# Pass two's score units moved next to pass one's, one addition moved from VectorE to GpSimd, and one early wait dropped

## What is computed

```python
xn  = layernorm(x)
# 1. rotary attention, 16 heads of 8, with a decay bias
q, k, v = heads(xn @ Wqkv.T);  q, k = rotate(q), rotate(k)
s   = q @ k.T / sqrt(8) - |i - j| / xi * e_g          # causal
a1  = (softmax(s) @ v) @ Wo.T
# 2. "soft mixture" attention: 8 experts gate the projections
n1  = layernorm(xn) * ln1_w + ln1_b;  rw = gating(n1)  # (tokens, 8)
q   = sum_e (n1 * rw_e) @ q_proj[e]   # k, v alike
hs  = xn + sum_e (softmax(q @ k.T / sqrt(128)) @ v * rw_e) @ o_proj[e]
# 3. mixture of 8 experts on the result
n2  = layernorm(hs) * ln2_w + ln2_b;  rw2 = gating(n2)
out = x + a1 + hs + sum_e (gelu(n2 @ w1[e]) @ w2[e]) * rw2_e
```

## Time and profile before

| | |
|---|---|
| median of 3 runs | 1262.35 us |
| the profiled execution | 1263.52 us, its span 1261.7 us |
| granted TensorE clock, mean | 0.985 |
| PE, PE weight load, DVE, ACT, POOL busy | 93%, 71%, 82%, 56%, 18% of the span |
| first matmul of step 0 / of the expert stage | 66.64 us / 1016.84 us |
| chain that ended last, by engine | PE 45%, DVE 29%, issue 15%, ACT 7%, the rest 4% |

### The profile page before, as it was taken

How to read it: one execution, slowest core, us unless ns; L and a number is a source line. 1 busy time by engine, 2 the same in 40 slices (tenths; PEclk the granted TensorE clock), 3 DMA queues, 4 the chain that set the end, 5 groups by cost and what they waited for, 6 DMA issues and landing times.

```text
span 1261.7 us, 33146 instructions
## 1 busy us (share of the span) xinstructions
PE 1177.7 (93%) x10652; PEld 899.4 (71%) x10652; DVE 1030.4 (82%) x3704; ACT 710.2 (56%) x1286; POOL 220.9 (18%) x338
## 2 busy tenths in 40 slices
PE   2399999999999999999999999999999899999998
PEld 1167777777777777777777777777777677777776
DVE  8878888888888888888888888888876667777664
ACT  2155565665666666655666666666665744555532
POOL 4212222222222222222222222222223000000000
PEclk9789999999999999999999999999999999999999
DMA  3433332333333333323323333333331044444453
GB/s 97 131 109 91 89 91 85 89 100 95 111 85 91 88 88 87 90 87 95 85 85 88 96 107 101 88 87 91 90 85 55 10 157 169 169 170 179 188 188 132
DMA packets 103113, 133.01 MB, mean 105 GB/s; under 512 B 13576, under 2 KB 82424, under 8 KB 94864
## 3 DMA queue, kind: packets, MB, share of 16 engines
q1 hardware_dynamic: 100548, 130.72, 33.3%
q10 hardware_dynamic: 2508, 1.58, 0.4%
HBM read 109.12 MB, written 21.54 MB: 104 GB/s over the span
## 4 chain that ended last, share of the span: by engine, by line
PE 45%; DVE 29%; issue 15%; ACT 7%; DVEq 3%; DMA 1%; POOL 0%; ACTq 0%; SPq 0%; POOLq 0%
PE ps L1838 9%; PE ps L1824 9%; PE ps L1621 4%; DVE mx L1175 3%; PE ps L1448 3%; PE ps L1552 3%; ACT ps L759 3%; ACT pr L753 3%; PE ps L1575 2%; PE ps L1576 2%; DVE rots L1100 2%; PE ps L1611 2%; DVE rots L1091 2%; PE ps L1585 1%; DVE rots L1095 1%
## 5 line engine op out<-in xcount | busy, mean ns | idle before, releaser
L753 ACT ACTIVATE pr<-ps 128x1024 f32<-128x1024 f32 x192 | 196.7, 1025 | 109.4 <-PE ps L1535 76.2
L1175 DVE TENSOR_REDUCE mx<-ps 128x4 f32<-128x1024 f32 (+1 forms) x192 | 234.9, 1224 | 20.1 <-PE ps L1508 12.0
L621 POOL TENSOR_TENSOR n1s<-rep,n1T 128x256 f32<-128x256 f32 x256 | 177.0, 729 | 299.5 <-DVE mpart L1189 279.5
L759 ACT ACTIVATE ps<-trn 128x1024 f32<-128x1024 bf16 x191 | 196.4, 1028 | 4.1
L1838 PEld LDWEIGHTS ps<-w2s,ats 128*128 128x128 f32 x1024 | 131.7, 192 | 51.2 <-issue 46.8
L1575 PE MATMUL ps<-n1s,wqk 128*128 128x256 f32 x512 | 163.7, 402 | 0.0
L1576 PE MATMUL ps<-n1s,wqk 128*128 128x256 f32 x512 | 153.2, 381 | 0.0
L950 ACT ACTIVATE n1s<-ps 128x512 f32<-128x512 f32 x128 | 76.5, 597 | 123.1 <-PE ps L1824 121.9
L1585 PE MATMUL ps<-wv,n1s 128*128 128x128 f32 x1024 | 141.6, 281 | 0.0
L1838 PE MATMUL ps<-w2s,ats 128*128 128x128 f32 x1024 | 135.7, 276 | 1.9 <-DVE ats L1378 1.9
L1585 PEld LDWEIGHTS ps<-wv,n1s 128*128 128x128 f32 x1024 | 126.7, 191 | 11.5 <-issue 6.5
(11 more groups left out here) (230 smaller groups left out, 2041.0 us busy)
## 6 DMA issues: line engine op xcount, KB each, us to landing
rep<-scr_rw SPq DMA_DIRECT2D x32, 1024.0 KB, 5.7
stk<-scr_rw SPq DMA_DIRECT2D x16, 1024.0 KB, 8.0
scr_parts<-parts SPq DMA_DIRECT2D x64, 192.0 KB, 5.8
stk<-scr_parts SPq DMA_DIRECT2D x248, 48.0 KB
rots<-scr_rw SPq DMA_DIRECT2D x8, 1024.0 KB, 4.7
wqk<-scr_rw SPq DMA_DIRECT2D x8, 1024.0 KB, 9.3
stk<-scr_parts SPq DMA_DIRECT2D x248, 32.0 KB
xt<-in_x SPq DMA_DIRECT2D x32, 128.0 KB, 2.1
```

The lines of the kernel that those rows point to most:

```text
L621: pool.tensor_tensor(n1s[:, e], rep[:, par, e], n1T[:, par], ALU.mult).then_inc(n1s_done, 1)
L753: act.activation(pr[:, Q, :, i], ps[:, S2[0]:S2[0] + NF], ACT.Exp).then_inc(exp_done, 1)
L759: act.activation(ps[:, S2[0]:S2[0] + NF], seeds[:, kind:kind + 1].broadcast_to((P, NF, 512)), ACT.Copy).then_inc(seed_done, 1)
L1175: dve.tensor_reduce(mx[:, min(i, 1)].rearrange("p (f h) -> p f h", f=NF)[:, :, h:h + n], ps[:, S1[0]:S1[0] + NF].rearrange("p f (h t) -> p ...
```

## The change

Three edits.

1. On PE, unit 3 of pass two now stands directly behind unit 3 of pass one (before `qk(n, 7)`), unit 4 directly behind unit 4 (before `soft_scores`, until now behind unit 5 of pass one), and unit 5 directly behind unit 5, with four of the eight `ve` behind it instead of one; `ve(n, 3)` goes ahead of unit 5 of pass one. On ACT exponential and seed 3 now stand ahead of `evac_qk`, and exponential and seed 4 ahead of `gate_tanh` and `soft_exp`.
2. The addition of `hs` and `xa` into `bs` leaves DVE's `add_hs` and becomes `add_base` on POOL, last in its step.
3. `scale(0, 0)` no longer waits for `max_chain`.

```diff
@@ gpsimd
-                pool.wait_ge(max_chain, (MAX_LINKS + 1) * (b + 1))
+                if not isinstance(b, int) or b:
+                    pool.wait_ge(max_chain, (MAX_LINKS + 1) * (b + 1))
...
+            def add_base(n, u):
+
+                pool.wait_ge(hs_done, n + 1)
+                pool.wait_ge(xa_done, n + 1)
+                pool.wait_ge(base_stored, 16 * n)
+                hv = hs[:, T * n:T * n + T] if isinstance(n, int) else hs[:, bass.ds(n * T, T)]
+                pool.tensor_tensor(bs[:, u], hv, xa[:, u], ALU.add).then_inc(base_done, 1)
+
             def step(n, u, n_x):
                 if n_x == 3:
                     second_norm(n + 3)
                 if n_x:
                     scale(n + 1, 1 - u)
+                add_base(n, u)
@@ scalar, step
+                exps(n, 3)
                 evac_qk(n)
-                exp_slot(n, 3)
                 evac_pv(n, 0)
-                seed_slot(n, 3)
+                exps(n, 4)
...
                 soft_exp(n)
-                exps(n, 4)
@@ vector, add_hs
-                dve.wait_ge(hs_done, n + 1)
-                dve.wait_ge(xa_done, n + 1)
-
-                dve.wait_ge(base_stored, 16 * n)
-                dve.tensor_tensor(bs[:, u], hv, xa[:, u], ALU.add).then_inc(base_done, 1)
@@ tensor, step
                 next_max(3)
+                unit2(n, u, 3)
                 qk(n, 7)
-                unit2(n, u, 3)
                 pv(n, u, 0)
...
                 next_max(4)
+                unit2(n, u, 4)
                 soft_scores(n)
                 ve(n, 0)
                 out_T(n, 0)
                 ve(n, 1)
                 ve(n, 2)
+                ve(n, 3)
                 next_max(5)
-                unit2(n, u, 4)
+                unit2(n, u, 5)
...
-                for e in range(3, 7):
+                for e in range(4, E):
                     ve(n, e)
-                unit2(n, u, 5)
-                ve(n, 7)
```

## The result

| | before | after |
|---|---|---|
| median (10 runs each) | 1262.03 us (1260.64 to 1263.69) | 1269.12 us (1265.28 to 1271.57) |
| the profiled execution, its span | 1263.5, 1261.7 us | 1271.0, 1268.9 us |
| ratio after to before | | 1.0053, 95% interval 1.0039 to 1.0067 |

The account below looks back on a forecast made before the run. PE, 93% busy, was taken to bound the kernel, plus one seed wait per step. Terms -22.3 + 1.5 + 1.3 - 1.3 = -20.8 us took 1263.5 to 1242.7, median 1.2 lower: 1241.5 us, range 1236 to 1253.

Parts of the forecast that it names:

- Edit 2: Addition moved from DVE to POOL: cost 0; if not hidden, DVE held up to 0.69 us per step.
- Margin for units 2 and 3: DVE starts `row_max(1)` earlier without its 0.43 us addition: margin for pass one's units, nothing off PE's path by itself.
- Edit 1, -22.3 us: Steady steps: PE's wait for ACT's seed before unit 5 of pass two goes entirely, -22.3 us; bounds 0 and -22.3.
- A step at PE's own 28.7 us: Steady steps: with the seed wait gone, a step of 29.62 us shrinks to PE's own 28.7 us.
- What is late next, +1.5 us: DVE's `row_max(5)` starts 0.43 us later, leaving `normalise(n, 1)` 0.1 us slack; PE waits in `att_T`, 0.05 for 30 steps.
- The start, +1.3 us: POOL's earlier products hold six small DVE operations, so the start ends 1.3 us later, between -1.6 and +2.2.
- The last step, -1.3 us: Step n = 31: less ACT work before `gate_tanh2(0)`, for which DVE waits; -1.3 us, gain at least 0, at most 1.77.
- D: Rival: DVE reaches `normalise(n, 1)` late after unit 5's hand-over, PE waits longer in `att_T`, 10 us slower, 1272; chance 0.06.

Follow-up runs that it names:

- Experiments 1 and 3: Four do-nothing memsets on DVE ahead of the steps: on the changed kernel (`pad4`), 1224.89 us; on the kernel before with edit 2 alone (`e2_pad4`), 1258.05 us.
- pad4: The changed kernel with four do-nothing memsets added on DVE ahead of the steps: 1224.89 us, ratio 0.9707 to the kernel before.
- no_e2: The changed kernel with the base's addition put back on DVE (edits 1 and 3 only): 1230.09 us, ratio 0.9745 to the kernel before.
- experiment 5: The run `apart`, units 3 and 5 of pass two moved away from those of pass one, against `pad4`: 1259.40 us.
- only_e2: The kernel before with edit 2 alone, the base's addition moved to POOL: 1304.04 us, ratio 1.0328 to the kernel before.
- e2_pad4: The kernel before with edit 2 alone, plus four memsets on DVE ahead of the steps: 1258.05 us, ratio 0.9964 to the kernel before.
- apart: `pad4` with unit 3 of pass two back behind `qk(n, 7)` and unit 5 behind one `ve`: 1259.40 us, ratio 0.9981 to the kernel before.

## Why the prediction was wrong

**The step that failed** is, under "Edit 2", "Cost 0; if it were not hidden it would hold DVE up to 0.69 per step". The operation was costed, its queue, its neighbour on the other engine, and all that was right: the addition takes 0.73 us on POOL, and the row maximum beside it still 1.22 to 1.23. What was left out is that removing instructions moves all that follow, and that the loop then began one or two instructions before a block's edge. Experiments 1 and 3 put 44 us on it in the new order and 46 in the old one. Step by step, between first and last `hs` update, the changed kernel takes 48.0 us more than `pad4`: the twelve steps behind the branch 389.7 us instead of 12 x 28.24 = 338.9, less 2.8 us in the steps between (27.95; why they are shorter no run showed). DVE's two stops make 45.4 us of it by the table of waits. The difference of the spans is 46.9.

**The sign of edit 2's work** was missed as well. "Margin for units 2 and 3" was worth 4 to 5 us: PE's weight loads did wait for row maxima, 0.3 to 0.7 us at a time, in a view (the waits of the weight load) that I had not read.

**Edit 1, -22.3 us.** The mechanism was right, in each place that the prediction named; the size was too small. What edit 1 does without edit 2 shows in `no_e2`, here two of its steps from one `hs` update to the next:

```profile
500.01:528.38 28.37, 28.15 (x287) 22.28 (x282) 26.29 (x96) 18.01 (x32) 6.49 (x10) 1.00 0.34 94
528.38:556.85 28.47, 28.17 (x288) 22.28 (x282) 26.03 (x96) 18.12 (x32) 6.53 (x10) 1.00 0.32 94
```

The step went from 29.62 and 29.30 to 28.47 and 28.37, 1.04 us on average, so some 31 over 30 steps. PE's idle time fell from 29.46 - 28.61 = 0.85 to 0.26, which is the forecast term: what PE waits for seeds is down from 22.3 us to 0.7 in all. The other 0.45 is PE's busy time, 28.61 to 28.16. "A step at PE's own 28.7 us" was the error: PE's own work is not the same in another order. Before, units 3 and 5 of pass two stood by themselves between f32 products (unit 5 at 529.65 in the earlier trace rows), and experiment 5 puts 0.1 and 0.3 us on that. The last 0.2 us of the step, to 28.2 in `pad4`, are the work of edit 2.

**What is late next, +1.5 us.** Right in place. PE waits for `att` 3.8 us in the changed kernel, more than twice the forecast, and in `pad4`, without DVE's stops, 5.8 us, of which 4.1 is one wait in the last step: 1.7 in all the others.

**The start, +1.3 us.** The mechanism is there, smaller. Beside POOL's product five small operations of DVE took 0.64 to 0.70, where six of 0.65 were forecast. The tanh starts at 56.89 instead of 54.64, 2.25 later and not 2.9, and the six DMA issues behind it took 2.96 instead of 3.32, so that `xzT` (62.01 in the earlier trace rows) starts at 62.40, not at 63.3:

```profile
47.44 5.48 POOL L622 TENSOR_TENSOR n1s<-rep,n1T 128x256 f32<-128x256 f32 x8 [16.44 <-DMA rep<-scr_rw]
...
56.89 0.22 ACT L736 ACTIVATE gt<-gt 128x16 f32<-128x16 f32 x1 [15.36 <-DVE gt L1135]
...
62.40 0.60 ACT L709 ACTIVATE xzT<-ps 128x512 f32<-128x512 f32 x1 [1.71 <-issue]
```

Step 0 begins 0.2 us later than before, and edit 3 can't be told from nothing in either kernel. Which operations are held is not told by the number of inputs: two of the five have one tensor input (L1006 and L104), and a two-input one (L112 at 49.46) took 0.15 beside the same product.

**The last step, -1.3 us.** It went from 38.11 to 35.43 us, so -2.7, and 35.14 in `pad4`. That is above my upper end, DVE's wait of 1.77, but PE's granted clock in this step was 0.87 before and 0.95 after. In `only_e2` and `e2_pad4`, which have the old order, the step took 37.97 us at 0.87 and 36.87 at 0.95, so about 1.1 of the 2.7 go with the clock and some 1.6 are left for the edit. I had not costed the clock.

**The rivals.** D gave 1272, close to what came, by a mechanism that did not: PE's new wait in `att_T` is 3.8 us, not 31 x 0.3 behind a late `row_max(5)`. A number near the result does not confirm a rival; the row that it names (`att`) has to carry it. With the loop in three blocks the forecast for the rest of the change would have been too high by 17 us: 1241.5 against 1224.9.

## What to carry to other kernels

Whoever adds or removes instructions ahead of or inside a hardware loop moves the whole loop, so look at the instruction queues in the profile's DMA list before and after, and for "issue" directly behind the backward branch; a few instructions that do nothing, in an idle place ahead of the loop, can be worth more than the edit. When a slowdown stands in every second step only, ask what happens every second step, before asking what the edit did. And test a failed edit with its side effect taken away: this one was a gain of 3%.

## What the runs showed of the hardware that I had not expected

- DVE's instructions come in packets of 8 KB, and the edges that the runs found fit 128 instructions to a packet. A loop of 345 stayed with the engine where it touched three such blocks, and was loaded again in each pass, five packets, where it touched four.
- Reached by a branch, a block that is not there stopped DVE for 2.25 us; where the next edge followed one or two instructions later there was a second stop, 1.8 us in the pass shown and 1.5 on average; with the edge 70 instructions later there was none.
- The stops come back on PE twice: as idle time (1.86 and 1.82 us), and in six of twelve passes as a lower granted clock (0.95 of full over the step, 0.50 in 496 to 498 us), with a pair of matmuls at 1.01 us instead of 0.6 to 0.7.
- Units of 64-row bf16 matmuls cost PE 0.1 to 0.3 us less when they stand next to each other than when each stands between f32 products (`apart` against `pad4`, units 3 and 5). Why was not tested.
- A tiny memset of 128x1 took 0.06 us on DVE, and 34 of them in an idle place changed nothing that can be measured (1223.6 us against 1224.3 to 1224.9).
